# Routing in a mixture of experts: scores transposed so that a partition holds one expert, ranks in one round, token ids laid out by TensorE

## What is computed

```python
xf = x.reshape(-1, h)                              # 4096 tokens x 256
scores = jax.nn.softmax(xf @ router_w + router_b)  # 4096 x 8
G, idx = jax.lax.top_k(scores.T, K)                # K = 512 tokens for each of 8 experts
toks = xf[idx]
h1 = jax.nn.relu(jnp.einsum('ekh,ehf->ekf', toks, w1) + b1[:, None, :])
eo = jnp.einsum('ekf,efh->ekh', h1, w2) + b2[:, None, :]
contrib = (eo * G[..., None]).reshape(-1, h)
y = jnp.zeros_like(xf).at[idx.reshape(-1)].add(contrib)
```

## Time and profile before

| what | us |
|---|---|
| median of 3 runs | 1333.94 (1333.66 to 1336.55) |
| the profiled execution | 1336.71 |
| its span | 1335.00 |
| end of attention and router, start of mixture's block | about 1033 |
| first hidden matmul | 1119.30 |
| last result matmul's end | 1316.87 |

### The profile page before, as it was taken

The page is one execution under the profiler, slowest core; times in us unless marked ns, Lnnn a source line. Parts: engine busy times, 40 slices in busy tenths (PEclk is TensorE's granted clock), DMA queues, the critical chain, the costliest instruction groups (busy, mean ns, idle before and its releaser), DMA issues. The chain is left out here.

```text
span 1335.0 us, 22038 instructions
## 1 busy us (share of the span) xinstructions
PE 1144.6 (86%) x7591; PEld 681.5 (51%) x7592; DVE 1017.3 (76%) x2733; ACT 680.2 (51%) x1359; POOL 518.5 (39%) x712
## 2 busy tenths in 40 slices
PE   4389999999999999999999999999995115999994
PEld 2255546455455554445454454544343004988984
DVE  4778778888888778889888898988852884766651
ACT  4015455554545555666656566666661103556551
POOL 6365563754748332324232323231021003445432
PEclk9569899998999999999999999999997556999997
DMA  5431523515345253342525252423111502545422
GB/s 172 108 85 43 112 76 87 120 39 111 81 111 121 78 123 83 101 105 79 112 65 112 65 111 75 102 71 74 34 48 34 161 1 96 163 111 109 112 23 26
DMA packets 90416, 118.06 MB, mean 88 GB/s; under 512 B 13057, under 2 KB 60161, under 8 KB 90178
## 3 DMA queue, kind: packets, MB, share of 16 engines
q1 hardware_dynamic: 84162, 108.12, 31.6%
q0 software_dynamic: 6144, 8.52, 3.8%
HBM read 48.76 MB, written 16.91 MB: 49 GB/s over the span
## 5 line engine op out<-in xcount | busy, mean ns | idle before, releaser
L739 ACT ACTIVATE probs<-ps_st 128x512 f32<-128x512 f32 (+3 forms) x1024 | 477.5, 518 | 345.9 <-PE ps_st L583 340.9
L601 PE MATMUL ps_p<-kst,qst 63*128 63x512 f32 (+3 forms) x1024 | 381.9, 435 | 10.9 <-DVE mx L827 8.3
L583 PE MATMUL ps_st<-qst,kst 64*128 64x512 f32 (+3 forms) x1024 | 358.6, 419 | 16.3 <-ACT probs L739 14.7
L825 DVE TENSOR_REDUCE mx<-ps_p 128x1 f32<-128x512 f32 x512 | 323.1, 681 | 19.7 <-PE ps_p L601 18.6
L583 PEld LDWEIGHTS ps_st<-qst,kst 64*128 64x128 f32 x1024 | 165.7, 188 | 267.1 <-ACT probs L739 206.7
L827 DVE CUSTOM_DVE_ANT_0 ps_p<-ps_p,tri 128x128 f32<-128x128 f32 (+3 forms) x512 | 238.5, 514 | 18.6 <-PE ps_p L601 15.6
L564 PE MATMUL ps_o<-probs,vals 128*32 128x512 f32 (+3 forms) x2048 | 234.6, 531 | 13.8 <-POOL probs L475 13.8
L601 PEld LDWEIGHTS ps_p<-kst,qst 63*128 63x128 f32 x1024 | 170.6, 190 | 40.4 <-DVE mx L827 17.8
L422 POOL TENSOR_SCALAR lnw<-mv 128x4 f32<-128x4 f32 x24 | 5.6, 234 | 346.5 <-DVE mv L811 346.5
L475 POOL TENSOR_SCALAR_AFFINE_SELECT probs<-probs 128x512 f32<-128x512 f32 x128 | 79.1, 633 | 91.8 <-ACT probs L739 91.8
L1189 PE MATMUL moe_ps_y<-moe_w,moe_hid_h 128*128 128x256 f32 x512 | 94.7, 283 | 0.0
(11 more groups left out here) (203 smaller groups left out, 1879.5 us busy)
## 6 DMA issues: line engine op xcount, KB each, us to landing
qst<-qk_h SPq DMA_DIRECT2D x64, 256.0 KB, 4.8
kst<-qk_h SPq DMA_DIRECT2D x64, 256.0 KB, 5.0
qst<-qk_l SPq DMA_DIRECT2D x32, 256.0 KB, 5.5
kst<-qk_l SPq DMA_DIRECT2D x32, 256.0 KB, 5.2
moe_w1r<-in_w_dram SPq DMA_DIRECT2D x8, 1024.0 KB, 5.2
moe_w2r<-in_w_dram SPq DMA_DIRECT2D x8, 1024.0 KB, 8.9
xin<-in_x_dram SPq DMA_DIRECT2D x8, 512.0 KB, 4.0
xres<-in_x_dram SPq DMA_DIRECT2D x8, 512.0 KB, 3.9
```

Of the source, the lines that this page charges most:

```text
L583: last = nc.tensor.matmul(out, kst[rows, t % 2, pair, kt * P:(kt + 1) * P], qst[rows, t % 2, pair, lo:S], start=True, stop=not masked)
L601: last = nc.tensor.matmul(ps_p1[:, i % 3, 0:keys], qst[rows, t % 2, pair, qt * P:(qt + 1) * P], kst[rows, t % 2, pair, 0:keys], start=True ...
L739: nc.scalar.activation(probs[:, kt, j, 0:n], ps_st[:, i % 2, 0:n], ACT.Exp, scale=float(DH) ** -0.5).then_inc(exp_done, 1)
L825: nc.vector.tensor_reduce(mx[:, g % 2, at:at + 1], bank, AX.X, ALU.max).then_inc(max_done, 1)
```

## The change

What it does, part by part:

- TensorE transposes the scores, so that partition 8 x (tile mod 16) + expert holds 128 tokens of one expert in each of 2 halves. The candidate is one number for each partition, the comparison and the count are one DVE instruction with an accumulator output, and the matmul adds the partitions of the same expert (matrix same). thr is one instruction. The 30 bits are written out with no loop.
- The ranks come from four flag passes with accumulators, five small matmuls for what lies before each partition, and four scans; two transposes turn the ranks back.
- TensorE spreads an expert's 32 x 16 ids over 128 partitions (spread_ids), and DVE picks and adds (column_ids) into ids. The DMA and SP's listed() are gone. For experts 2 to 7, spread_ids and column_ids stand at ft 4.
- DVE waits for gathers_begun, which GpSimd raises after gather(0), before it splits expert 0's weights; it splits two pieces before the tokens and two after. TensorE waits for two pieces before hidden and for all four at ft 2.

```diff
             weights(0)
             weights(1)
             sp.wait_ge(scored, 1)
...
-            listed(0)
-            listed(1)
             for e in range(2, E_N):
                 weights(e)
-                listed(e)
...
             gather(0)
+            pool.sem_inc(gathers_begun, 1)
             gather(1)
```

TensorE:

```diff
+            for h in range(2):
+                last = nc.tensor.transpose(ps_a[:, 0, h * P:(h + 1) * P], logits[:, h * NT // 2:(h + 1) * NT // 2, :].rearrange("p t e -> p (t e)"), ident[:, :])
+            last.then_inc(score_turned, 1)
+            for k in range(BITS):
+                pe.wait_ge(cnt_ready, k + 1)
+                nc.tensor.matmul(ps_h[:, 0, 0:1], same[:, :], cnt[:, :], start=True, stop=True).then_inc(cnt_sum, 1)
+            pe.wait_ge(sums_ready, 1)
+            nc.tensor.matmul(ps_h[:, 1, 0:4], same_before[:, :], sums[:, :, :].rearrange("p k h -> p (k h)"), start=True, stop=False)
+            for k in range(2):
+                nc.tensor.matmul(ps_h[:, 1, 2 * k + 1:2 * k + 2], same[:, :], sums[:, k, 0:1], start=False, stop=(k == 1))
+            for h in range(2):
+                last = nc.tensor.matmul(ps_h[:, 0, 0:1], same[:, :], sums[:, 0, h:h + 1], start=(h == 0), stop=(h == 1))
+            last.then_inc(begins_ready, 1)
+            pe.wait_ge(rank_ready, 1)
+            for h in range(2):
+                last = nc.tensor.transpose(ps_a[:, 1, h * P:(h + 1) * P], rank[:, h, :], ident[:, :])
+            last.then_inc(place_turned, 1)
...
+            def spread_ids(e):
+                pe.wait_ge(id_ready, e + 1)
+                nc.tensor.matmul(ps_a[:, 0, 64:64 + LO], spread[:, :], id_tok[:, e % 2, :], start=True, stop=True).then_inc(id_spread, 1)
...
             for e in range(E_N):
-                pe.wait_ge(w_low, 4 * (e + 1))
+                pe.wait_ge(w_low, 4 * e + 2)
...
                     hidden(e, ft)
+                    if ft == 2:
+                        pe.wait_ge(w_low, 4 * e + 4)
...
                         list_ids(e + 2)
+                    if e + 2 < E_N and ft == 4:
+                        spread_ids(e + 2)
```

VectorE:

```diff
+            with nc.allow_low_precision("zeros and ones"):
+                link(nc.vector.tensor_reduce(own_row[:, :], identb[:, :].rearrange("p (t e) -> p e t", e=E_N), AX.X, ALU.max))
+            nc.vector.tensor_copy(same[:, :].rearrange("p (t e) -> p t e", e=E_N), own_row[:, :].unsqueeze(1).to_broadcast([P, P // E_N, E_N]))
...
+            dve.wait_ge(score_turned, 1)
+            link(nc.vector.tensor_copy(score[:, :, :], ps_a[:, 0, 0:2 * P].rearrange("p (h k) -> p h k", h=2)))
+            for k in range(BITS):
+                bit = 1 << (BITS - 1 - k)
+                with nc.allow_low_precision("counts up to 256 are exact"):
+                    nc.vector.tensor_scalar(out=ge[:, :, :], in0=score[:, :, :], scalar1=cand[:, 0:1].bitcast(F32), scalar2=0.0,
+                                            op0=ALU.is_ge, op1=ALU.add, accum_out=cnt[:, :]).then_inc(cnt_ready, 1)
+                link(nc.vector.tensor_scalar(out=thr[:, :], in0=cand[:, :], scalar1=bit, scalar2=bit >> 1,
+                                             op0=ALU.bitwise_xor, op1=ALU.bitwise_or))
+                dve.wait_ge(cnt_sum, k + 1)
+                link(nc.vector.tensor_scalar(out=won[:, :], in0=ps_h[:, 0, 0:1], scalar1=float(CAP), scalar2=float(bit),
+                                             op0=ALU.is_ge, op1=ALU.mult))
+                link(nc.vector.tensor_tensor(out=cand[:, :], in0=thr[:, :], in1=won[:, :], op=ALU.bitwise_or))
+            limit = cand[:, 0:1].bitcast(F32)
+                for i, (flags, op) in enumerate(((above, ALU.is_gt), (tied, ALU.is_equal))):
+                    for h in range(2):
+                        last = nc.vector.tensor_scalar(out=flags[:, h, :], in0=score[:, h, :], scalar1=limit, scalar2=0.0,
+                                                       op0=op, op1=ALU.add, accum_out=sums[:, i, h:h + 1])
...
+            link(nc.vector.tensor_tensor(out=same_before[:, :], in0=same[:, :], in1=before[:, :], op=ALU.mult))
+            dve.sem_inc(sums_ready, 1)
+            link(nc.vector.tensor_reduce(quarter[:, :], ident[:, :].rearrange("p (k j) -> p j k", j=4), AX.X, ALU.max))
+            dve.wait_ge(begins_ready, 1)
+            nc.vector.tensor_scalar(out=need[:, :], in0=ps_h[:, 0, 0:1], scalar1=-1.0, scalar2=float(CAP), op0=ALU.mult, op1=ALU.add)
+            link(nc.vector.tensor_copy(begins[:, :, :], ps_h[:, 1, 0:4].rearrange("p (k h) -> p k h", k=2)))
+            for i, (up, flags) in enumerate(((up_tied, tied), (up_above, above))):
+                for h in range(2):
+                    last = nc.vector.tensor_tensor_scan(out=up[:, h, :], data0=one[:, :], data1=flags[:, h, :],
+                                                        initial=begins[:, 1 - i, h:h + 1], op0=ALU.mult, op1=ALU.add)
...
+            link(nc.vector.tensor_scalar(out=place[:, :, :], in0=ps_a[:, 1, 0:2 * P].rearrange("p (t e) -> p e t", e=E_N),
+                                         scalar1=-1.0, scalar2=None, op0=ALU.add))
...
+            def column_ids(e):
+                q = e % 2
+                dve.wait_ge(id_spread, e + 1)
+                link(nc.vector.tensor_tensor(out=id_wide[:, q, :].rearrange("p (j c) -> p j c", j=4),
+                                             in0=ps_a[:, 0, 64:64 + LO].rearrange("p (j c) -> p j c", j=4),
+                                             in1=quarter[:, :].unsqueeze(2).to_broadcast([P, 4, 4]), op=ALU.mult))
+                with nc.allow_low_precision("one of four is not zero"):
+                    nc.vector.tensor_reduce(ids[:, e, :], id_wide[:, q, :].rearrange("p (j c) -> p c j", j=4), AX.X,
+                                            ALU.add).then_inc(ids_ready, 1)
...
             one_hots(0)
             take_ids(0)
+            column_ids(0)
             one_hots(1)
             take_ids(1)
-            for part_ in range(4):
-                low_w(0, part_)
+            column_ids(1)
+            dve.wait_ge(gathers_begun, 1)
+            for half in range(2):
+                low_w(0, half)
             for k in range(KT):
                 low_tokens(0, k)
+            for half in range(2, 4):
+                low_w(0, half)
...
                         take_ids(e + 2)
+                    if e + 2 < E_N and ft == 4:
+                        column_ids(e + 2)
```

More of the change, by code:

```diff
@@ L966, in mixture @@
         HI, LO = 32, 16
-        BITS, UNROLL = 30, 6
-        SC = E_N * NT
+        BITS = 30
         top = sb("top", [P, NT], F32)
         tot = sb("tot", [P, NT], F32)
[L971 to L984, removed]
+        score = sb("score", [P, 2, P], F32)
+        ge = sb("ge", [P, 2, P], BF16)
+        thr = sb("thr", [P, 1], I32)
+        cand = sb("cand", [P, 1], I32)
+        won = sb("won", [P, 1], I32)
+        cnt = sb("cnt", [P, 1], BF16)
+        above = sb("above", [P, 2, P], F32)
+        tied = sb("tied", [P, 2, P], F32)
+        sums = sb("sums", [P, 2, 2], BF16)
+        begins = sb("begins", [P, 2, 2], F32)
+        need = sb("need", [P, 1], F32)
+        up_above = sb("up_above", [P, 2, P], F32)
+        up_tied = sb("up_tied", [P, 2, P], F32)
+        picked = sb("picked", [P, 2, P], F32)
+        rank = sb("rank", [P, 2, P], F32)
         place = sb("place", [P, E_N, NT], I32)
@@ L987, in mixture @@
         place_lo = sb("place_lo", [P, E_N, NT], I32)
-        ones = sb("ones", [P, P], BF16)
+        one = sb("one", [P, P], F32)
         before = sb("before", [P, P], BF16)
+        own_row = sb("own_row", [P, E_N], BF16)
+        same = sb("same", [P, P], BF16)
+        same_before = sb("same_before", [P, P], BF16)
+        spread = sb("spread", [HI, P], F32)
+        quarter = sb("quarter", [P, 4], F32)
         iota = sb("iota", [P, HI], I32)
@@ L1082, in _ @@
             for op in (
-                lambda: nc.gpsimd.memset(ones[:, :], 1.0),
+                lambda: nc.gpsimd.memset(one[:, :], 1.0),
                 lambda: nc.gpsimd.memset(before[:, :], 1.0),
@@ L1297, in _ @@
-            with dve.Fori(0, BITS // UNROLL) as i:
-                for u in range(UNROLL):
-                    bit_step(i * UNROLL + (u + 1), u % 2, i * (STEPS * UNROLL) + (base + STEPS * u))
-            n[0] = base + BITS * STEPS
-            def at_thr():
-                return cand[:, :].bitcast(F32).unsqueeze(2).to_broadcast([P, E_N, NT])
-            link(nc.vector.tensor_tensor(out=above[:, :, :], in0=score[:, :, :], in1=at_thr(), op=ALU.is_gt))
-            nc.vector.tensor_tensor(out=tied[:, :, :], in0=score[:, :, :], in1=at_thr(), op=ALU.is_equal).then_inc(pre_in, 1)
```

109 lines of the change are left out of this document (33 added, 76 removed).

## The result

The changed kernel takes 1317.16 us (median of 4 runs, 1316.14 to 1317.85), the kernel before beside it 1333.80 (4 runs): a ratio of 0.987, 95% interval 0.9856 to 0.9883, or 16.6 us less. Forecast were 20.8 us less and 1313.1, in a range of 1307 to 1321.

A forecast was written before the change was run, and what follows sets the result against it. Routing latency before the experts, then PE in the experts, was taken as the bound, earlier starts counting one for one; +0.8 - 13.2 - 1.3 - 1.9 - 6.1 + 0.9 = -20.8 us from 1333.9 gave 1313.1, range 1307 to 1321.

The forecast's parts named there:

- the experts' stage grows by over 3: One of two signs that the forecast is wrong; the other was the stages before the experts shrinking by less than 13 us.
- The bits: Threshold's 30 bits: fused compare and count, no loop, 1.19 us a bit in place of 1.56; -13.2 us (-16.5 to -11.4).
- I take 0.51: Within a bit: compare with accumulator has its count after 0.51 us, just under the custom operation's 0.52.
- 0.28 for the trip through TensorE: Within a bit: the time for the count's trip through TensorE's matmul, 0.28 us of the 1.19.
- Before the bits: Scores up to the first compare: two f32 transposes, hand-overs and a PSUM copy add 0.8 us (0.4 to 1.2).
- bits to places: From last bit to places: flag passes, small matmuls, scans and transposes take 7.1 us for 8.39; -1.3 (-2.3 to +0.5).
- Ids without a DMA: Expert 0's ids to its first gather: matmul, product, reduce and hand-over take 0.9 us for 2.81; -1.9 (-2.2 to -1.3).
- The gathers: First gather's issue to landing: splits no longer hold an issue, landing takes 3.1 us; 8.2 for 14.3, -6.1 (-7.8 to -1.0).
- rival 3: Semaphore after gather(0) may rise once issues are queued; splits start at T+6 and hold gather 4; 1316 to 1319, 17%.
- In the experts: Experts' stage: six spread_ids join PE's stream, +0.9 us (0.5 to 1.8); column_ids on DVE hides.
- 0.15 each: Experts' stage: each spread_ids matmul costs PE 0.15 us, some 0.11 at the high clock plus a break in the stream.
- rival 4: Slower than before: spread_ids in PE's queue at ft 4 waits for take_ids on DVE; 1338 if 6 us late; 3%.

The follow-up runs named there:

- no_split: Changed kernel with its last part undone: expert 0's four weight splits in one row, no DVE wait for a gather, TensorE waits for all four pieces; 1318.79 us.
- ids_two: Changed kernel with spread_ids and column_ids for experts 0 and 1 alone, ids of experts 2 to 7 by SP's DMA; 1313.19 us.
- splits_only: Kernel before with the last part alone: semaphore, two splits before the tokens, two after, TensorE's two waits; 1326.90 us.
- unroll_only: Kernel before with its 5-turn loop for the 30 bits written out on DVE and TensorE, nothing else; 1332.0 us (1 run).
- no_wait: Changed kernel without the semaphore gathers_begun, neither raised by GpSimd nor waited for by DVE; 1315.0 us (1 run).
- warm: Changed kernel with twelve extra unused bf16 matmuls, six after spread_ids(0) and six after spread_ids(1), where TensorE idles; 1316.73 us.
- best: Changed kernel with TensorE ids for experts 0 and 1 alone, plus twelve extra unused matmuls while TensorE idles; 1312.18 us (5 runs).
- gapped: Kernel before with only the scores, bits and ranks part, plus a DVE wait on itself behind each of expert 0's four splits; 1315.5 us (1 run).
- halves_row: Kernel before with only the scores, bits and ranks part, each of expert 0's four splits as two halves, eight in a row; 1320.8 us (1 run).
- halves_gap: Kernel before with only the scores, bits and ranks part, expert 0's splits as eight halves, a DVE wait behind each; 1318.1 us (1 run).

## Why the prediction was right, point by point

The total lies in the range because errors partly cancelled, and one of the forecast's own signs of being wrong came up: "the experts' stage grows by over 3". It grew by 3.7. The other did not: the stages before the experts shrank by 20.4, where 13 was the limit.

- **What bounds the kernel.** Right: the 20.4 us won before the first hidden matmul came off the end, less the 3.7 that the experts took.
- **The bits**, -13.2 forecast, -11.5 measured. The mechanism was right, and so was the term "I take 0.51" for compare and count: the read ends after 0.49. The mis-sized term is "0.28 for the trip through TensorE": from the count to won it is 0.35, since won starts 0.30 after the matmul where it had started 0.23 after it. The whole bit is 1.23 in place of 1.19, 1.2 us over 30. Why the answer comes later is open. The first bit took 0.35 more, which no step had; why is open.
- **Before the bits** and **bits to places**: +0.6 and -1.4 for +0.8 and -1.3, right.
- **Ids without a DMA**, -1.9 forecast, -0.7 measured over the stage from place_hi. Two terms were mis-sized. The f32 matmul was taken at the 0.36 of one row; it is two passes, 0.60. The hand-over to GpSimd was taken as small as DVE's; it is 0.92 (1084.02 to 1084.94). The kernel before had it too: its DMA landed at 1100.52, the gather began at 1101.45.
- **The gathers**, -6.1 forecast, -7.3 measured, and here the sum hid a wrong step. "The change puts the splits behind a semaphore that GpSimd raises after gather(0), so that hold goes": the semaphore rises early, as rival 3 had it, and the hold goes with no semaphore too (no_split 7.1). What moved the splits away from the four issues was column_ids and the ids' earlier arrival. They began at T+6.3, as rival 3 had it; its price didn't fall due because the fourth issue had begun 0.11 sooner, which is luck as far as the forecast goes. "The first held by hot_lo": it took 1.30, against 1.23 for the first issue before, so it was hardly held where 1.5 had been allowed, and the fourth issue started 4.2 after the first, not 5.1. The landing took 2.8 for the 3.1 forecast, which was right, and so was the reason (weights(2) comes later, at 1097.65).
- **In the experts**, +0.9 forecast, +3.7 measured: the step "0.15 each" is 0.51 each, six times, 3.2 by ids_two. The row it was taken from was misread: the x16 of the earlier trace rows counts passes, and L622 issues 8 matmuls in that window (two token tiles by two halves of the channels, twice), so a matmul there took two steps of 0.22 and not one. At the high clock that is 0.22, measured 0.32, and the break behind it is 0.19 more. The other 0.5 is the later rise of the clock, which no term had.
- **Slower than before** (rival 4): TensorE never waited for id_tok in the experts. Right.

The errors that cost most, 1.7 in the bits, 1.2 in the ids and 2.8 in the experts, had one sign; the gathers gave 1.2 back, by a mechanism other than the forecast's. The measured 1317 lies where the forecast had put rival 3, for another reason.

## What to carry to other kernels

The issue of an indirect DMA on GpSimd can be held as long as DVE runs operations with two SBUF inputs without a gap between them; look for issues that take longer than their neighbours and end a fixed time after DVE's row, and put a wait of DVE on itself between such operations before you rearrange the order of work. Two parts of a change that remove the same stall are not worth their sum: run each alone and each left out, since here, on top of the first part, the ids part was worth 5.7 us and beside the splits part -1.9. A price read from a row needs the row's count checked against the kernel: 16 records were 8 matmuls. What shortens a path once should be done once: the same step, repeated in a stage where its engine is the bound, cost 3 us of what it had won.

## What had not been expected of the hardware

- A semaphore that GpSimd raises behind four indirect DMAs in its program has risen when the first has been issued (by 1100.60 in splits_only), 4.6 us before the fourth issue ends (1105.16).
- The hold: 0.83 us from the end of DVE's row to the issue's end in four kernels (5.25, 5.26, 4.57 and, in unroll_only, 4.28 long), with a gap of 0.04 us enough to let the issue in. In seven others the issue got in at the first change between two splits that it met, without a gap, and ended 0.82 to 0.83 after the split that had held it; what decides between the two is open.
- From ready ids to the start of GpSimd's first indirect DMA 0.92 us pass, be it a DMA or DVE that made them.
- DVE idled 2.1 us more before take_ids(1) in no_wait, ids_two, warm and best, marked "remote", and not in the changed kernel, though TensorE's matmuls had ended: it went on 0.07 to 0.10 before the end of GpSimd's fourth issue. In unroll_only, gapped, halves_row and halves_gap it went on 0.12 to 0.16 after the first issue's end, 0.3 later than in the rest. What it waited for is open.
